# Turning the gathered rows by a transposing DMA instead of TensorE, and stacking the last chunk of the shared down projection

## What is computed

```python
shared = shared + _swiglu(x, sh_gate[i], sh_up[i], sh_down[i])      # i in 0, 1; F = 352
w, sel = jax.lax.top_k(probs, K)                                    # K = 2 of 8
routed = routed + Wte[:, e:e + 1] * _swiglu(x, exp_gate[e], exp_up[e], exp_down[e])
# _swiglu = silu(x @ wg) * (x @ wu) @ wd
```

## Time and profile before

| | us |
|---|---|
| median of three runs | 382.75 (382.38 to 382.76) |
| the profiled execution | 382.96 |
| its span (first to last instruction) | 380.9 |
| PE busy | 362.4 (95%) |
| DVE / ACT / POOL busy | 238.6 / 166.6 / 155.8 |
| routed experts in steady state | 217.34 to 334.07 of the span, 35 steps |

### The profile page before, as it was taken

The page is one execution under the profiler, slowest core; times in us unless marked ns, Lnnn a source line. Parts: engine busy times, 40 slices in busy tenths (PEclk is TensorE's granted clock), DMA queues, the critical chain, the costliest instruction groups (busy, mean ns, idle before and its releaser), DMA issues.

```text
span 380.9 us, 7891 instructions
## 1 busy us (share of the span) xinstructions
PE 362.4 (95%) x2671; PEld 222.6 (58%) x2672; DVE 238.6 (63%) x594; ACT 166.6 (44%) x286; POOL 155.8 (41%) x241
## 2 busy tenths in 40 slices
PE   7998999999999999889999899999999999999992
PEld 2354444454454555455446677777777777766570
DVE  1367999776657547787774455565556556546574
ACT  1145377467655675451441333333333333322560
POOL 3000564656537631000020365565565556422652
PEclk9999999999999999999999999999999999999997
DMA  7975213433353410100000122222222222213922
GB/s 232 391 289 202 75 41 108 147 114 113 129 179 98 141 55 2 56 2 0 2 28 2 42 85 83 69 83 81 71 81 83 82 70 83 69 43 138 353 90 109
DMA packets 18037, 39.24 MB, mean 103 GB/s; under 512 B 2976, under 2 KB 9376, under 8 KB 17888
## 3 DMA queue, kind: packets, MB, share of 16 engines
q1 hardware_dynamic: 13552, 28.71, 22.2%
q0 software_dynamic: 3744, 10.23, 8.5%
q10 hardware_dynamic: 720, 0.02, 0.1%
HBM read 29.65 MB, written 9.31 MB: 102 GB/s over the span
## 4 chain that ended last, share of the span: by engine, by line
PE 73%; DVE 16%; issue 3%; ACT 3%; DMA 2%; POOL 1%; POOLq 0%; ACTq 0%; SPq 0%; DVEq 0%
PE bank L998 57%; PE bank L1145 7%; PE bank L1243 3%; DVE prod L903 2%; DVE x L776 2%; PE bank L1227 2%; PE bank L1014 2%; ACT acts L581 2%; DMA x<-wc 2%; DVE x L891 1%; DVE w0s L646 1%; DVE acts L908 1%; DVE hs L634 1%; ACT sil L571 1%; PE bank L1074 1%
## 5 line engine op out<-in xcount | busy, mean ns | idle before, releaser
L442 POOL TENSOR_TENSOR w1s<-piece,w1s 128x170 f16<-128x170 f32 x128 | 61.6, 520 | 78.5 <-ACT piece L531 78.5
L998 PE MATMUL bank<-w0s,hs 128*128 128x512 f16 x384 | 86.2, 379 | 1.4 <-DVE x L776 1.2
L998 PE MATMUL bank<-w1s,rT 128*128 x468 | 76.2, 313 | 1.5 <-DVE rT L962 1.5
L451 POOL DMA_INDIRECT rows<-token_store,row_in x39 | 38.0, 974 | 88.2 <-DVE row_in L873 48.5
L776 DVE SCALAR_TENSOR_TENSOR x<-bank,coef,x 128x256 f32<-128x256 f32 x128 | 54.8, 478 | 19.3 <-PE bank L998 19.0
L998 PEld LDWEIGHTS bank<-w0s,hs 128*128 128x128 f16 x384 | 36.9, 98 | 44.1 <-DVE x L776 1.9
L998 PE MATMUL bank<-hs,w1s 128*128 128x512 f16 x264 | 59.3, 379 | 1.9 <-DVE prod L903 1.9
L998 PEld LDWEIGHTS bank<-w1s,rT 128*128 128x128 f16 x468 | 44.0, 98 | 22.0 <-issue 2.0
L456 POOL DMA_INDIRECT results<-yb,row_out x39 | 38.6, 990 | 37.0 <-ACT yb L605 37.0
L998 PE MATMUL bank<-w1s,aT 128*128 (+1 forms) x351 | 44.8, 272 | 0.8 <-DVE aT L955 0.8
L599 ACT ACTIVATE ract<-prod 128x352 f16<-128x352 f32 x39 | 19.4, 498 | 58.4 <-DVE prod L968 33.6
(11 more groups left out here) (149 smaller groups left out, 405.4 us busy)
## 6 DMA issues: line engine op xcount, KB each, us to landing
piece<-w SPq DMA_DIRECT2D x16, 680.0 KB, 3.9
w1s<-results SPq DMA_DIRECT2D x6, 512.0 KB, 9.4
x<-wc SPq DMA_DIRECT2D x4, 512.0 KB, 6.7
w1s<-xT SPq DMA_DIRECT2D x4, 512.0 KB, 10.2
w1s<-w SPq DMA_DIRECT2D x4, 512.0 KB, 8.8
token_store<-xrow SPq DMA_DIRECT2D x4, 512.0 KB, 2.9
out<-x SPq DMA_DIRECT2D x8, 256.0 KB, 2.0
x<-x SPq DMA_DIRECT2D x1, 1536.0 KB, 10.6
```

The lines of the kernel that those rows point to most:

```text
L442: ins = nc.gpsimd.tensor_tensor(w1s[:, LO, at], piece[:, i % 2, part], w1s[:, HI, at], ALU.subtract)
L451: pool.indirect_dma_start(rows[:, i % 2], None, token_store, bass.IndirectOffsetOnAxis(row_in[:, i:i + 1], 0)).then_inc(s_row[i % 2], 16)
L998: mm = nc.tensor.matmul(out_ap, l, r, start=(i == 0), stop=(i == len(terms) - 1))
```

## The change

The gathered rows are turned by one transposing DMA for each tile, issued by SP, straight from `rows` into `rT`; TensorE's row transposes (L1227), VectorE's copy (L962), `s_ra` and `s_rx` go. SP issues the DMA of tile i when the gather has landed (`s_row`) and gate and up of tile i - 2 are done (`s_ru`), and gate and up of tile i wait for it (`s_turn`). `rows` has four buffers, so a gather is issued up to five tiles ahead and waits for the turn of tile i - 4. TensorE's wait on `s_acc` before the first step becomes one on `s_prod`.

In the shared down projection VectorE writes the last chunk's LO half to rows 64 to 127 of the HI tile, and the weights' rows 0 to 63 of that chunk are repeated in rows 64 to 127. HI x HI and LO x HI become one pass of 128 rows, so the chunk has two passes, not three (the second also adds LO x LO).

In the diff below the parts are, in order: constants and buffers, the weights' view, SP's queue, POOL's gathers, the LO half on VectorE, VectorE's step, the down projection, TensorE's step, the wait before the first step, and the host's layout of the weights.

```diff
+    DOWN_PASSES = [((HI, HI), (LO, HI), (HI, LO))] * (ST - 1) + [((HI, HI), (HI, LO))]
+    AHEAD = 4
...
-        rows = sb("rows", [P, 2, ROW], F16)
+        rows = sb("rows", [P, AHEAD, ROW], F16)
...
-            return w1s[0:SR[f], hl, o:o + D]
+            return w1s[:, hl, o:o + D]
...
+            for i in range(TILES):
+                sp.wait_ge(s_row[i % AHEAD], 16 * (i // AHEAD + 1))
+                if i >= 2:
+                    sp.wait_ge(sm["s_ru"], i - 1)
+                sp.dma_start_transpose(rT[:, i % 2].rearrange("p a k n -> p (a k) n"), rows[:, i % AHEAD]
+                                       ).then_inc(s_turn[i % 2], 16)
...
             def fetch(i):
-                if i >= 2:
-                    pool.wait_ge(sm["s_ra"], i - 1)
-                pool.indirect_dma_start(rows[:, i % 2], None, token_store,
-                                        bass.IndirectOffsetOnAxis(row_in[:, i:i + 1], 0)).then_inc(s_row[i % 2], 16)
+                if i >= AHEAD:
+                    pool.wait_ge(s_turn[i % 2], landed(i - AHEAD, i % 2))
+                pool.indirect_dma_start(rows[:, i % AHEAD], None, token_store,
+                                        bass.IndirectOffsetOnAxis(row_in[:, i:i + 1], 0)
+                                        ).then_inc(s_row[i % AHEAD], 16)
...
-            for s in range(-4, TILES + 1):
-                if known(s + 4):
-                    fetch(s + 4)
+            for s in range(-1 - AHEAD, TILES + 1):
+                if known(s + 1 + AHEAD):
+                    fetch(s + 1 + AHEAD)
                 if known(s - 1):
                     put(s - 1)
...
-                nc.vector.tensor_tensor(acts[0:M, c % 2, f, LO], prod[0:M, p], acts[0:M, c % 2, f, HI],
+                low = acts[:, c % 2, f, LO] if f < ST - 1 else acts[REST:2 * REST, c % 2, f, HI]
+                nc.vector.tensor_tensor(low, prod[0:M, p], acts[0:M, c % 2, f, HI],
...
-                i = s + 2
-                if known(i):
-                    dve.wait_ge(sm["s_ra"], i + 1)
-                    if again(i):
-                        dve.wait_ge(sm["s_ru"], i - 1)
-                    nc.vector.tensor_copy(rT[:, par].rearrange("p a k n -> p (a k n)").bitcast(F32),
-                                          bank[4][:, 0:D]).then_inc(sm["s_rx"], 1)
...
-                            for n, (a, b) in enumerate(PASSES):
+                            for n, (a, b) in enumerate(DOWN_PASSES[f]):
                                 mm = nc.tensor.matmul(bank[4 + q][:, 0:D],
-                                                      acts[0:SR[f], c % 2, f, a, q * P:(q + 1) * P], w_dn(b, f),
-                                                      start=(f == 0 and n == 0), stop=(f == ST - 1 and n == 2))
+                                                      acts[:, c % 2, f, a, q * P:(q + 1) * P], w_dn(b, f),
+                                                      start=(f == 0 and n == 0), stop=(f == ST - 1 and n == 1))
...
-                i = s + 2
-                if known(i):
-                    pe.wait_ge(s_row[par], landed(i, par))
-                    if isinstance(i, int) and i == 1:
-                        pe.wait_ge(sm["s_rx"], i)
-                    for a in range(2):
-                        for k in range(KT):
-                            o = (a * KT + k) * P
-                            mm = nc.tensor.transpose(bank16[4][:, o:o + P], rows[:, par, o:o + P], ident16[:])
-                    mm.then_inc(sm["s_ra"], 1)
...
                 i = s + 2
                 if known(i):
-                    pe.wait_ge(sm["s_rx"], i + 1)
+                    pe.wait_ge(s_turn[par], landed(i, par))
+                    if again(i):
+                        pe.wait_ge(sm["s_rprod"], i - 1)
...
-            pe.wait_ge(sm["s_acc"], TPB + 1)
+            pe.wait_ge(sm["s_prod"], EARLY)
...
+        dn[g.shape[1]:] = dn[full:g.shape[1]]
```

More of the change, by code:

```diff
@@ L255, in build_program @@
             "s_acc",
-            "s_ra",
-            "s_rx",
             "s_rg",
@@ L282, in build_program @@
         s_piece = [sem(f"s_piece{c}") for c in range(NP)]
-        s_row = [sem(f"s_row{c}") for c in range(2)]
+        s_row = [sem(f"s_row{c}") for c in range(AHEAD)]
+        s_turn = [sem(f"s_turn{c}") for c in range(2)]
         s_put = [sem(f"s_put{c}") for c in range(2)]
```

## The result

The changed kernel took **393.93 us** (median of four runs, 391.93 to 394.08) beside 382.75 before (382.38 to 384.39): ratio 1.0249, 95% interval 1.0216 to 1.0282. It is slower where I forecast faster (370.0), and above my range (366 to 390). That was one session on one chip. In a later session, on chip 2, the same kernel took **371.63** (369.28 to 372.80, six runs) beside 382.87 before: 0.9681, 0.9645 to 0.9717. So there are two results for one program. Their traces say where they part; the experiments tell how I came, late, to look.

A forecast was written before the change was run, and what follows sets the result against it. The prediction took TensorE's order of work, busy 95% of the span, as the bound. Gains of 7.9 (steps), 1.4 (start) and 3.6 (downs) sum to 12.9 us: 382.96 to 370.1, median 370.0; range 366 to 390 for 8 in 10.

The forecast's parts named there:

- Part 1: Routed experts, steady state: without row transposes a step falls from 3.335 to 3.12 us, gaining 7.9 us over 36 steps.
- Part 2: Transposing DMA's new wait: with two `rT` buffers, hidden behind TensorE's work while its latency is under 4.45 us; 3.4 expected.
- the margin that I had worked out for `aT`: Routed step: `aT` is ready at 260.13, down needs it at 260.48 in the shorter step; 0.35 us spare.
- all that I had not thought of: Chance 0.03 for something else that costs about what is gained.
- Rival B: Gate and up wait for the turn, which becomes the bound; slower kernel, such as 390, 393 or 414 us; chance 0.20.
- the sum: Whole kernel: gains of 7.9 + 1.4 + 3.6 = 12.9 us, between 9.5 and 16.9.
- L: Time from end of gate and up of tile i - 2 to DMA-allowed start of tile i's; 3.4 us forecast.
- A: The turn is a little late, L between 4.45 and 5.0; 376.9 us at 4.75; chance 0.15.
- C: The turn's four blocks go one by one, 8.4 us a turn, step 5.1; 445 us in all; chance 0.08.
- Part 3: Start of routed work: tile 2's gate and up 5.2 us after down(1), gaining 1.4 us (0.3 to 2.7).
- Part 4: Stacked chunk in shared down: 1.2 us gained in each of three downs, 3.6 in all (1.3 to 6.3).
- rival D: Shared down: idles beside the last chunk stay, so it gains 1.3, not 3.6; 372.3 us; included in forecast's 0.54.

The follow-up runs named there:

- e1: Kernel before with only the stacked last chunk of the down projection, rows still turned by TensorE; 380.10 us, ratio 0.9911 (chip 7).
- e2: e1 plus a transposing DMA per tile into a spare buffer nobody reads, and POOL's wait for it; 388.72 us, ratio 1.0145 (chip 7).
- e17: The changed kernel itself, unchanged, run again on chip 2; 371.63 us, ratio 0.9681.
- e9: Changed kernel, but POOL's wait before a gather is for TensorE's gate of tile i - 4, not its turn; 369.93 us, ratio 0.9669 (chip 2).
- e12: Changed kernel with plain scatters of 128 consecutive rows, indirect gathers kept; 369.89 us (chip 2).
- e13: Changed kernel, POOL waiting before a gather first for gate of tile i - 4, then for its turn; 370.09 us (chip 9).
- e15: Changed kernel with each gather issued one step later, POOL still waiting for the turn; 369.94 us (chip 9).
- e18: The version of e9 run again beside e17 on chip 2; 369.54 us, ratio 0.9662.
- e8: Changed kernel with plain DMAs of 128 consecutive rows for gathers and scatters, still issued by POOL; 369.63 us (chip 14).
- e11: Changed kernel with plain gathers of 128 consecutive rows by POOL, indirect scatters kept; 368.64 us (chip 2).
- e7: Changed kernel with plain DMAs issued by SP for gathers and scatters, POOL issuing nothing in the routed part; 367.39 us (chip 14).
- e5: e2 with a plain SBUF to SBUF copy of 128 KB as the spare DMA; 383.96 us, ratio 1.0009 (chip 14).
- e6: e2 with a plain copy of 4 KB a tile as the spare DMA; 384.05 us, ratio 0.9997 (chip 14).
- e14: e1 with one more POOL wait before a gather, for a gather long landed, no DMA added; 379.16 us (chip 9).

## Why the prediction was wrong, and what of it was right

The step that failed is in parts 1 and 2: "None of them becomes the bound" and "The semaphore waits added on TensorE cost nothing while their producers are early". Both take it that a semaphore is raised when its instruction ends. In the first session TensorE's own were up to 2.7 us late, and the margin that I had worked out for `aT` was 0.35 us. So the wait of TensorE that grew is not at `rT` but at `aT`, where TensorE waits for a copy that waited for TensorE. Price: a mean step of 135.64 / 36 = 3.77 where 3.12 was forecast, 36 x 0.65 = 23.4 us. No rival had it; I gave 0.03 to all that I had not thought of. Rival B has the right sign with the wrong mechanism.

That e1, on a chip where the additions bring lateness, has none shows that the change provokes it there: a DMA per tile in SP's queue, and POOL's wait for it, beside the indirect ones (e2). How it does so no run shows, and that part of the cause stays open.

Everything else can be tested on e17, where updates are on time. Its profiled execution took 371.96 against 382.96, a span of 370.2 against 380.9: 10.7 us where the sum said 12.9.

*Part 1.* The step is 3.11 or 3.12 in 33 of 36, as forecast, but three are longer (4.21, 3.58, 3.38) and cost 1.84 together. Gain 120.11 - 113.87 = 6.2, not 7.9. The longest is in the chain of waits on chip 2:

```profile
210.13 0.02 issue
210.15 0.02 SPq L392
210.16 0.05 issue
210.21 2.41 DMA rT<-rows
212.62 0.12 issue
...
217.85 0.02 SPq L392
217.87 0.03 issue
217.90 5.17 DMA rT<-rows
223.06 0.13 issue
```

The first turn is the normal case: 2.41 us from issue to landing, in L = 212.75 - 210.13 = 2.6, the lower half of my estimate (3.4; 2.1 to 4.5). The second took 5.17; L is then 223.19 - 217.85 = 5.34 and gate and up of tile 5 start late, by 1.1. A third, issued at 299.89, took 4.54 and made the step of 3.58. The DMA view of 219 to 223.5 shows the queues' share of the engines then, where the steady share is 0.47 in all:

```profile
q0 software_dynamic: 142, 0.39, 56.5%
q1 hardware_dynamic: 1084, 0.26, 42.8%
q8 instruction: 1, 0.02, 2.2%
```

Gathers, scatters and two turns fill the engines wholly, about a load of instructions of 16 KB. That this load starts it is not tried, and it is not the whole: every trace with the changed step on chips 2, 9 and 14 has such a load between 216.9 and 220.9, but tile 5's step is 3.95 to 4.34 with indirect gathers (e9, e12, e13, e15 to e18), 3.33 with POOL's plain ones (e8, e11) and 3.11 in e7. At 299.89 there is no such load.

*Part 2.* L fits under 4.45 in steady state with 1.8 us to spare; TensorE waited for the turned rows for 1.2 us in all. Rivals A and C fall with it, and B in its own mechanism. The turn was the cheap thing here: in e8's DMA view its median is 2.5 us, issued by SP in 1.19:

```profile
rT<-rows SPq DMA_TRANSPOSE x39, 2.5
rows<-token_store POOLq DMA_DIRECT2D x39, 128.0 KB, 2.4
results<-yb POOLq DMA_DIRECT2D x39, 128.0 KB, 2.0
```

The two plain DMAs of the same 128 KB, from and to HBM, take 2.4 and 2.0. The Trainium skill (VectorE: DVE Perf Modes, The three transpose paths) gives 1309 ns a block of 128 x 128, four of which in series would be 5.24; the measured 2.5 for four blocks disagrees with them in series, and the measurement decides.

*Part 3.* Tile 2's gate and up start 4.58 after tile 0's, not 5.2: 2.05 gained for 1.4, since L was 2.6 and not 3.4 (against that, tile 0's gate and up end after 1.97, not 1.79).

*Part 4.* TensorE's down(2), before and then on chip 2:

```profile
346.96 8.75 PE L1145 MATMUL bank<-w1s,acts 128*128 128x256 f16 x72
355.65 1.68 PE L998 MATMUL bank<-hs,w1s 128*128 128x512 f16 x7
...
338.26 7.59 PE L1147 MATMUL bank<-w1s,acts 128*128 128x256 f16 x68
345.68 9.23 PE L1000 MATMUL bank<-hs,w1s 128*128 128x512 f16 x42
```

7.42 us from start to start, where before took 355.65 - 346.96 = 8.69; 1.27 for the 1.2 forecast, and no idle at the last chunk, which in down(0) now shows as 30 loads in a row where the earlier trace rows breaks at 15 and 3:

```profile
166.89 3.18 PEld L1147 LDWEIGHTS bank<-w1s,acts 128*128 128x128 f16 x30 [1.65 <-issue]
```

So rival D falls. Up to the start of the routed work two downs should bring 2.4; e17 shows 208.65 - 208.16 = 0.49, because of something older (the last section); in e18, which does not have it, those steps start at 206.48, 2.2 earlier. The stretch from tile 38 to the end gives 45.5 - 43.6 = 1.9: 1.2 of it before down(3) as forecast, and 0.7 behind its start. That 0.7 is not down(3)'s, which ends at 362.73, while VectorE's last accumulation starts at 365.39; it is off the path, as I had it. POOL's last four additions took 4.81 in the earlier trace rows and here, as in e1,

```profile
360.07 3.42 POOL L478 TENSOR_TENSOR x<-x,w1s 128x256 f32<-128x256 f32 x4 [2.47 <-ACT w1s L626]
```

and the span ends 6.7 after them in both kernels. Why they were slower in the one trace of before no run shows.

The sum on chip 2: 0.5 + 2.05 + 6.2 + 1.9 = 10.7 in place of 12.9, and 12.4 without the 1.7 us of the clock told below. That 12.4 lies so near 12.9 is in part luck: part 1 brought 1.7 less than forecast, part 3 brought 0.65 more, and POOL's additions 0.7 that no term had. Of e17's six runs the two fastest took 369.28 and 369.61, on my 370.0. On chip 2 the working was right about the work; it was silent about the signals, on which the first session turned.

## What to carry to other kernels

A control that comes out the same on every chip does not show that the chips are the same: the kernel before took 382.3 to 384.6 everywhere, while the changed one took 394 and 372. Before any theory of a surprise, run the surprising kernel itself again, beside the version that seems to cure it, on one chip; I did so last, and eight runs had been read against a number from another chip. And in a forecast, look at how large the margin is at each wait that becomes tight (0.35 us at `aT`), not only at the new one: it is there that lateness of any source shows, whatever its cause.

## What the runs showed of the hardware

- TensorE's semaphore updates can come up to 2.7 us after the end of their instruction, in 32 to 64% of those recorded, while VectorE's and ScalarE's do not. It was seen in three sessions of six, only in kernels with indirect gathers, indirect scatters, a DMA of SP in each step and POOL's wait for that DMA; all these executions were recorded ones. A DMA of 4 KB does as much as one of 128 KB (e5, e6).
- A transposing DMA of a whole 128 x 512 tile of fp16 is 544 packets (q1 has 34768 in e17 and 13552 in e14, over 39 tiles), and its median to landing is 2.4 us in e7 and 2.5 in e8, with single ones up to 3.9 and 4.3, and 5.17 in e17. Plain DMAs of 128 KB from and to HBM took 2.4 and 2.0 in e8.
- TensorE ran at its lower level for a few matmuls in some executions. The windows view (granted clock third from the end) of 34 to 38 us in e17, then in before:

```profile
34.00:38.00 4.00, 4.00 (x12) 1.47 (x11) 1.54 (x5) 1.65 (x2) 0.00 (x0) 0.58 0.80 327
```

```profile
34.00:38.00 4.00, 4.00 (x20) 1.96 (x19) 3.24 (x7) 1.53 (x2) 0.00 (x0) 1.00 0.77 310
```

12 matmuls for 20, near the level of 1.2 GHz. From there e17 is about 1.7 us behind e18, which has not got it; in the 4 us before, TensorE is busy for 2.39 us in both of the traces shown. After in the first session has it as well (0.61). The runs of before lie in two groups, near 382.5 and near 384.3; a step of 1.8 us like this one would make them, but no trace of the upper group of before is kept. Two other kernels bear it out: e14's runs lie near 378.2 and near 380.0, its trace is of the upper group (380.05) and has the lower level there (0.57), and e1's is of its lower group (378.37, the other near 380.1) and has not (1.00).
